# The scaled layer-2 output stays in its PSUM bank, and the final addition reads it there

## What is computed

```
h   = relu(layernorm(x))                      # no scale, no shift
agg = segment_sum(edge_attr, src)             # over 50000 nodes
z   = silu(concat([h, agg]) @ W1 + b1)        # 256 -> 256
y   = z @ W2 + b2                             # 256 -> 128
ln  = (y - mean(y)) * rsqrt(var(y) + 1e-5) * ln_gamma + ln_beta
out = x + (ln + h)
```

## Time and profile before

| | |
|---|---|
| median of 3 executions | 801.94 us (800.46 to 802.87) |
| profiled execution | 803.43 us, span 801.9 us |
| PE busy | 733.6 us (91%) |
| DVE busy | 732.1 us (91%) |
| ACT busy | 587.0 us (73%) |
| POOL busy | 601.1 us (75%) |
| L430 gathers (POOL) | 392, mean 1124 ns |
| L418 copies (POOL) | 392, mean 354 ns |
| L886 `scale` (DVE) | 392, mean 341 ns |
| L896 `result` (DVE) | 98, mean 681 ns |

### The profile page before, as it was taken

One profiled execution on the slowest core, in us unless ns is written; L12 is line 12 of the kernel. 1 busy time (PEld: TensorE's weight loads), 2 busy tenths in 40 slices (PEclk: granted clock), 3 DMA queues, 4 the chain that ended last, 5 costly groups with the idle time before them and its releaser, 6 DMA issues.

```text
span 801.9 us, 15882 instructions
## 1 busy us (share of the span) xinstructions
PE 733.6 (91%) x4567; PEld 592.4 (74%) x4616; DVE 732.1 (91%) x2494; ACT 587.0 (73%) x1927; POOL 601.1 (75%) x831
## 2 busy tenths in 40 slices
PE   4999993989999999999999999999999999989990
PEld 1455542878888888888888888888888888878880
DVE  6999995879999999999999999999999999989994
ACT  4999982767777777777777777777777777757860
POOL 4600006889998999889989998999989998989920
PEclk9999995999999999999999999999999999999996
DMA  5000000122323333332323232323233332321211
GB/s 191 2 1 2 1 0 17 48 74 75 124 90 110 98 103 99 102 120 80 126 74 126 74 125 74 127 78 121 91 107 100 102 107 93 126 66 51 71 61 48
DMA packets 28159, 65.86 MB, mean 82 GB/s; under 512 B 8379, under 2 KB 9934, under 8 KB 28070
## 3 DMA queue, kind: packets, MB, share of 16 engines
q1 hardware_dynamic: 15526, 51.90, 18.6%
q0 software_dynamic: 12544, 12.93, 6.5%
HBM read 51.98 MB, written 25.60 MB: 97 GB/s over the span
## 4 chain that ended last, share of the span: by engine, by line
POOL 66%; ACT 10%; issue 8%; PE 8%; DVE 5%; DMA 1%; SPq 0%; POOLq 0%; DVEq 0%
POOL G L430 50%; POOL gather_rows L418 16%; ACT junk_rank L472 10%; PE y L630 2%; PE za L602 1%; PE pre L613 1%; PE pre L614 1%; DVE hot_tile L768 1%; PE pre L618 1%; DVE hot_slot L790 1%; DVE T L886 1%; DMA srci<-in_src_dram 1%; DMA G<-in_edge_attr_dram,gather_rows 1%; PE za L595 0%; DVE is_slot L781 0%
## 5 line engine op out<-in xcount | busy, mean ns | idle before, releaser
L430 POOL DMA_INDIRECT G<-in_edge_attr_dram,gather_rows x392 | 440.6, 1124 | 63.4 <-POOL gather_rows L418 48.2
L418 POOL COPY gather_rows<-slot_edge 128x1 uint32<-128x1 uint32 x392 | 138.5, 354 | 92.0 <-DVE slot_edge L842 89.6
L630 PE MATMUL y<-w2c,S 128*128 128x128 f32 x1568 | 190.9, 275 | 3.3
L630 PEld LDWEIGHTS y<-w2c,S 128*128 128x128 f32 x1568 | 191.5, 192 | 2.5
L493 ACT ACTIVATE H<-X,shift,rstd 128x128 f32<-128x128 f32 x392 | 162.4, 508 | 7.7 <-DVE shift L752 7.6
L613 PE MATMUL pre<-hi,w1h 128*128 128x512 f32 x392 | 164.8, 420 | 0.4 <-issue 0.4
L870 DVE TENSOR_TENSOR lo<-za,hi 128x1024 fp32r<-128x1024 f32 x98 | 119.8, 1222 | 46.5 <-ACT hi L502 42.3
L614 PE MATMUL pre<-hi,w1l 128*128 128x512 f32 x392 | 156.1, 398 | 0.0
L500 ACT CAST hi<-za 128x512 fp32r<-128x512 f32 x98 | 57.4, 586 | 123.5 <-PE za L595 113.6
L602 PE MATMUL za<-HOT,G 128*128 128x128 f32 x784 | 114.4, 290 | 18.4 <-issue 10.1
L508 ACT ACTIVATE S<-pre,b1c 128x512 f32<-128x512 f32 x196 | 125.3, 697 | 5.0 <-remote 2.1
(11 more groups left out here) (123 smaller groups left out, 1047.3 us busy)
## 6 DMA issues: line engine op xcount, KB each, us to landing
X<-in_x_dram SPq DMA_DIRECT2D x48, 512.0 KB
out_dram<-R SPq DMA_DIRECT2D x48, 512.0 KB
G<-in_edge_attr_dram,gather_rows POOLq DMA_INDIRECT x392
X<-in_x_dram SPq DMA_DIRECT2D x1, 424.0 KB
out_dram<-R SPq DMA_DIRECT2D x2, 212.0 KB
w1f<-in_L_gnn_W_dram SPq DMA_DIRECT2D x1, 256.0 KB, 3.3
w2f<-in_L_gnn_W_dram SPq DMA_DIRECT2D x1, 128.0 KB, 2.6
srci<-in_src_dram SPq DMA_DIRECT2D x1, 97.2 KB
```

Of the source, the lines that this page charges most:

```text
L418: nc.gpsimd.tensor_copy(gather_rows[b.xj][:, t:t + 1], slot_edge[:, bass.ds(b.number(TILES, t), 1)]).then_inc(row_named, 1)
L430: nc.gpsimd.indirect_dma_start(G[b.j][:, t, :], None, source, bass.IndirectOffsetOnAxis(ap=gather_rows[b.xj][:, t:t + 1], axis=0), bounds_ ...
L630: done = nc.tensor.matmul(place[:, t * D:(t + 1) * D], S[c][:, m, t * P:(t + 1) * P], w2c[:, m, :], start=False, stop=(t == HALF - 1 and m ...
```

## The change

Three edits. `scale` writes its product back over its own input, in the PSUM bank of `y`, in place of the SBUF tile `T`, which is gone. `result` therefore has one input in PSUM (`y`) and one in SBUF (`R`), where it had two in SBUF. And since the bank is now read by `result`, `layer2` waits for `out_done` in place of `t_done` before it writes that bank two blocks later. The count that it waits for is the same, and no instruction is added, removed or moved on any engine.

```
-        T = [sb(f"T{c}", [P, HALF, D], F32) for c in range(2)]
...
-                at_least(pe, t_done, b.half(c, 1, -3))
+                at_least(pe, out_done, b.half(c, 1, -3))
...
                     done = nc.vector.scalar_tensor_tensor(
-                        out=T[c][:, t, :], in0=y[2 * b.ring(2) + c][:, t * D:(t + 1) * D],
+                        out=y[2 * b.ring(2) + c][:, t * D:(t + 1) * D], in0=y[2 * b.ring(2) + c][:, t * D:(t + 1) * D],
                         scalar=rstd[b.j][:, n:n + 1], in1=gammas[:], op0=ALU.mult, op1=ALU.mult)
...
-                nc.vector.tensor_tensor(out=R[b.j][:, s, :], in0=T[c][:], in1=R[b.j][:, s, :],
+                nc.vector.tensor_tensor(out=R[b.j][:, s, :], in0=y[2 * b.ring(2) + c][:].rearrange("p (t d) -> p t d", d=D),
+                                        in1=R[b.j][:, s, :],
                                         op=ALU.add).then_inc(out_done, 1)
```

## The result

The changed kernel took 772.85 us (median of 4 runs, 768.83 to 773.29) against 802.4 us for the kernel before (800.46 to 803.43 in 4 runs); the ratio is 0.962, with a 95% interval of 0.959 to 0.966. The forecast was 775 us. The profiled execution has a span of 771.7 us, 30.2 us under that of before.

What follows compares the result with a forecast made beforehand. POOL was taken as the bound at 13.11 us a block; freed, DVE sets 12.38 + 0.02 + 0.09 = 12.49 us. Over 41 blocks that saves 28.3 us, less 1.3 for a late gather: 801.94 - 27 = 775 us, range 768 to 798.

Steps and rivals of the forecast that it cites:

- What bounds the kernel: POOL, issuing eight gathers a block, sets the pace at 13.11 us; alone it would need 11.1 us.
- Part 1, the hold: `result`: two SBUF inputs on DVE hold POOL up; reading PSUM ends that, costing DVE 0.02 us a block.
- The walk: POOL's reads stepped through DVE's block: without L896's hold, eight gathers fit 12.38 us; before, seven.
- the walk's rule for a held copy: POOL: a held copy ends 0.04 us after the DVE instruction that held it.
- Part 2, the PSUM write: `scale` (L886) writing PSUM costs zero; starts stay 0.259 us apart; each 0.01 us would cost 0.08 us a block.
- Both rivals that rested on a price here: `scale`'s PSUM write costs a part, 790 us (18%), or so much that DVE's block lengthens, some 820 us (10%).
- Part 3, the release: PE's bias matmul (L626) waiting for `out_done` costs zero: the first `result` ends 3.8 us before it.
- The sum: 41 blocks of 12.49 us take 512.1 for 540.4; with 1.3 us of late gather, 27 us less.
- The late gather: One gather PE awaited 3.25 us at 719.53; up to 2.9 us may show again, 1.3 taken.
- The hold that takes another place: Rival: the gather reading 0.09 us ahead of L878 loses; block near 13.0 us, 798 to 802 us; 14%.
- A mixed operand that still holds POOL: Rival: `result` with one PSUM operand still holds the port, no effect, 802 us; 2%.

Runs made afterwards that it cites:

- the read alone: Kernel before with the later bank release and `result` reading PSUM, `scale` still writing T in SBUF: ratio 1.004 on the first chip, 0.956 (765.8 us) on the second.
- the write alone: Kernel before with the later bank release and `scale` writing PSUM, `result` still adding zero-filled T from SBUF: 1.002 on the first chip, 0.999 (802.8 us) on the third.
- first-half kernel: Changed kernel with only half c=0 kept in PSUM; half c=1, the second addition, still goes through T in SBUF: 804.9 us, ratio 1.002 to the kernel before.
- the profile of the second chip: The changed kernel run once more, unaltered, on the second chip: 768.95 us, ratio 0.958 to the kernel before.
- second-half kernel: Changed kernel with only half c=1 kept in PSUM; half c=0, the first addition, still goes through T in SBUF: 772.2 us, ratio 0.962 to the kernel before.

## Why the prediction was right

**What bounds the kernel.** POOL's issue set the pace: on the third chip, taking its copies away, and nothing else, brought the block to 12.29 us.

**Part 1, the hold.** Shown: the read alone has the gain (0.956, second chip), the write alone none (0.999, third chip). L895's own time, for which I had added 0.01 us, did not change: two occupy 1.20 us (609.84 to 611.04), as in the earlier trace rows. The 0.13 us a block that the prediction estimated for a dearer PSUM source are not borne out.

**The walk.** It told which of the two additions matters, and both half-changes came out in time as walked, though in the first-half kernel the copy was held through L878 too, which the walk's rule for a held copy doesn't give. Two more details were off. I had put 0.09 us of DVE time on the gather that reads just ahead of L878: at 610.84 it started 0.20 us ahead of the L877 at 611.04, took 1.03 us, and L877 its 0.68, so neither paid. And DVE's block is not 12.38 us but 12.28 (606.04 to 618.32): the stretch from the second one-hot to the first L852 takes 3.05 us where it took 3.11 in the earlier trace rows, and that to the second 0.68 for 0.70. PE's transposes are 12.29 us apart there as in the earlier trace rows:

```profile
603.20 0.47 PEld L594 LDWEIGHTS za<-ident,H 128*128 128x128 f32 x4
...
615.49 0.47 PEld L594 LDWEIGHTS za<-ident,H 128*128 128x128 f32 x4
```

so PE and DVE are now level, and no run tells which of them sets the 12.29.

The step that was off in its size is the one that let every block run in the walked pattern from the start. Within the first 16 blocks DVE still waited ten times for ACT's `hi`, as here, and the second one-hot caught a gather in place of a copy:

```profile
223.63 1.22 DVE L869 TENSOR_TENSOR lo<-za,hi 128x1024 fp32r<-128x1024 f32 x1 [0.26 <-ACT hi L501]
...
225.02 0.68 DVE L860 TENSOR_TENSOR HOT<-iota_node,slot_node 128x512 f32<-128x512 f32 x1
```

```profile
225.31 1.29 POOL L429 DMA_INDIRECT G<-in_edge_attr_dram,gather_rows  x1 [0.16 <-POOL gather_rows L417]
```

A block took 12.66 us there. My walk had DVE without waits as its frame; there the gathers were still awaited, `lo` came later, and with it the second one-hot, into other reads of POOL (read from the trace; no run tests it). Slower early blocks and faster late ones made a mean of 12.48 where 12.49 was forecast: the agreement of the mean is partly luck. When the short blocks set in isn't fixed by the program: in the profile of the second chip they began some eight blocks sooner, and that execution took 769.4 us where this one took 773.3:

```profile
338.80 0.68 DVE L860 TENSOR_TENSOR HOT<-iota_node,slot_node 128x512 f32<-128x512 f32 x1
...
682.99 0.68 DVE L860 TENSOR_TENSOR HOT<-iota_node,slot_node 128x512 f32<-128x512 f32 x1
```

These are 28 blocks of 12.29 us (344.2 / 28).

**Part 2, the PSUM write.** Zero, as taken. The row grew from 341 to 351 ns, but eight instructions occupy 2.07 us as before (607.77 to 609.84 against 185.17 to 187.24 in the earlier trace rows). Both rivals that rested on a price here (790 and 820 us) fall.

**Part 3, the release.** Free, as forecast.

**The sum.** From the one-hot of block 7 to that of block 48: 512.7 us (212.38 to 725.11), forecast 512.1 and 1.3 us (up to 2.9) for the late gather; before 540.4. The late gather is there in the changed kernel too, and PE waited 1.41 us for it instead of 3.25:

```profile
691.13 0.97 PEld L601 LDWEIGHTS za<-HOT,G 128*128 128x128 f32 x8 [1.41 <-DMA G<-in_edge_attr_dram,gather_rows]
```

Another 2.8 us (215.18 to 212.38) lie ahead of that stretch, where I had put nothing, and they aren't shown to be the change's: in the profile of before ACT and then DVE stood at 167.64 and 169.73 with nothing that the profile names (the rows above), and the block there took 17.01 us. The first-half kernel, which gains nothing, has no such wait and reaches the same one-hot at 212.18, the write alone at 213.93. The tail is 46.6 us for 46.3. Together 27.7 + 2.8 - 0.3 = 30.2 us, the difference of the spans.

**The rivals.** The hold that takes another place didn't come: the gather ahead of L877 ran its 1.03 us. That a single hold can take the whole gain is real, though: leaving only the second addition in SBUF did it. A mixed operand that still holds POOL is ruled out by the read alone.

## What to carry to other kernels

When POOL's gathers set the pace, look at which of its rows are longer than its undisturbed ones and what DVE runs at that moment; an operand that could stay in PSUM took an instruction out of its way here at no cost of its own (0.60 us and 0.259 us from start to start, as before). Count holds by where the other engine reads, not by their number: half of this change had all of the gain or none. And ask first whether the held engine needs its extra instructions: without the 392 copies the change was worth nothing, and the kernel of before without them (760.9 us) was 8 us faster than the changed kernel on the same chip (768.7).

## What the runs showed of the hardware

In the cases seen, a gather of POOL was sensitive only near its start: those that started 0.40 and 0.20 us ahead of a DVE addition with two SBUF inputs ran their 1.03 us (604.43 in the second-half kernel, 610.84 in the changed one), one that started 0.04 us ahead of a one-hot took 1.66 us. Whether a held copy is let in between two such instructions without a gap isn't settled: of three in a row it was let in behind the second (0.69 us, in the kernel before), of two in a row it was held through both (1.29 us, in the first-half kernel), each time having come 0.03 us behind the start of the one that held it. Behind a small instruction between them it was let in, as at the two L852 above. DVE's start-to-start time was the same with a PSUM or an SBUF destination (0.259 us for 128 columns, PSUM source) and with one PSUM input or none (0.60 us for 512 columns). And the same program gained 4.4% on one chip and nothing on another.
